# A decoder of two layers on one core: the last pair's routing and its scatter move behind the attention, the shared experts' operands are loaded inside it, and three of eight shared units run beside the first routed experts

## What is computed

```
x = x + L0_attn(layernorm(x));  x = x + L0_xattn(layernorm(x), ctx)
x = x + L0_ffn(layernorm(x))                      # 8 experts, top 2, and a shared one
x = x + L1_attn(layernorm(x));  x = x + L1_xattn(layernorm(x), ctx, 16 heads of 64)
x = x + L1_ffn(layernorm(x))                      # below

scores = sigmoid(x @ gate.T); choose 4 of 8 groups of 8 experts, then top 8 of 64 experts
xe[e, pos] = x[token]   for the first 256 tokens of each expert e
ye = (silu(xe @ w1.T) * (xe @ w3.T)) @ w2.T                       # hidden size 128
out[token] += 2.5 * weight * ye[e, pos]
shared = silu(x @ shared_gate.T) * (x @ shared_up.T) @ shared_down.T   # hidden size 256
```

## Time and profile before

| | |
|---|---|
| median of 3 runs | 3784.36 us (3773.11 to 3792.74) |
| the profiled execution | 3764.9 us, span 3763.2 us |
| busy | PE 3304.6 us, DVE 1865.9, ACT 1650.9, POOL 846.2 |
| granted TensorE clock, mean | 0.952 |

### The profile page before, as it was taken

How to read it: one execution, slowest core, us unless ns; L and a number is a source line. 1 busy time by engine, 2 the same in 40 slices (tenths; PEclk the granted TensorE clock), 3 DMA queues, 4 the chain that set the end, 5 groups by cost and what they waited for, 6 DMA issues and landing times. The chain is left out here.

```text
span 3763.2 us, 76649 instructions
## 1 busy us (share of the span) xinstructions
PE 3304.6 (88%) x24490; PEld 2470.7 (66%) x24491; DVE 1865.9 (50%) x5115; ACT 1650.9 (44%) x4558; POOL 846.2 (22%) x920
## 2 busy tenths in 40 slices
PE   5999996899999777499996988999999999959882
PEld 4777775666666554277774766777777777746762
DVE  3555553677777642022221663556565665642333
ACT  2555553666666410022221325666656565621220
POOL 0000000000000033133332110132323233241774
PEclk9999998999999888799998999999999999979996
DMA  8400003000000231111112000010000000012885
GB/s 275 114 0 0 0 0 135 11 10 8 10 9 10 88 85 48 19 31 30 29 29 55 0 18 27 16 39 19 18 12 12 15 11 13 10 57 90 225 212 138
DMA packets 152369, 181.52 MB, mean 48 GB/s; under 512 B 46428, under 2 KB 126425, under 8 KB 151276
## 3 DMA queue, kind: packets, MB, share of 16 engines
q1 hardware_dynamic: 102476, 137.64, 12.3%
q0 software_dynamic: 47808, 26.74, 4.4%
q10 hardware_dynamic: 2016, 16.25, 1.0%
HBM read 116.17 MB, written 103.88 MB: 58 GB/s over the span
## 5 line engine op out<-in xcount | busy, mean ns | idle before, releaser
L1203 DVE TENSOR_REDUCE e_nmx<-PS 128x1 f32<-128x361 f32 x416 | 221.2, 532 | 400.4 <-PE PS L1044 384.8
L1554 ACT ACTIVATE b_p<-PS,b_nmx 100x361 f32<-100x361 f32 x512 | 275.5, 569 | 162.4 <-DVE b_nmx L1641 162.4
L847 POOL DMA_INDIRECT slot_rows<-r_row,r_rows_now x256 | 255.7, 999 | 401.2 <-DVE e_p L1210 274.8
L1044 PE MATMUL PS<-e_cT,e_qT 128*128 128x361 f32 x832 | 330.1, 479 | 0.0
L1150 ACT ACTIVATE e_pT<-PS 121x384 f32<-121x384 f32 (+1 forms) x416 | 199.2, 479 | 226.2 <-PE PS L1051 219.4
L1641 DVE TENSOR_REDUCE b_nmx<-PS 100x1 f32<-100x361 f32 x512 | 247.5, 526 | 97.6 <-PE PS L1404 95.8
L2509 PE MATMUL PS<-c_wgu,c_tile_xT 128*128 x912 | 290.5, 462 | 1.3 <-ACT c_tile_xT L2564 1.3
L1051 PEld LDWEIGHTS PS<-ident,e_p 128*121 128x121 f32 x1248 | 199.7, 186 | 96.6 <-issue 1.1
L1155 ACT ACTIVATE e_p<-PS,e_nmx 128x361 f32<-128x361 f32 x416 | 232.6, 559 | 69.4 <-DVE e_nmx L1203 67.4
L2754 POOL DMA_INDIRECT sum<-f_y,f_y_token x128 | 198.8, 1553 | 124.0 <-issue 111.6
L1411 PE MATMUL PS<-ident,b_p 100*121 100x100 f32 x1536 | 221.6, 280 | 5.4 <-PEq L181 2.7
(11 more groups left out here) (325 smaller groups left out, 6477.5 us busy)
## 6 DMA issues: line engine op xcount, KB each, us to landing
f_w<-in_f_W SPq DMA_DIRECT2D x64, 384.0 KB
slot_rows<-a_empty SPq DMA_DIRECT2D x1, 21504.0 KB, 65.1
f_xg<-slot_rows SPq DMA_DIRECT2D x64, 336.0 KB
c_wgu<-in_c_GU ACTq DMA_DIRECT2D x8, 1408.0 KB, 19.0
sum<-X SPq DMA_DIRECT2D x2, 3200.0 KB, 57.2
f_sums<-sum SPq DMA_DIRECT2D x16, 400.0 KB
b_cT<-in_ctx_T SPq DMA_DIRECT2D x32, 181.5 KB, 2.3
e_cT<-in_ctx_T SPq DMA_DIRECT2D x32, 181.5 KB, 2.4
```

The lines of the kernel that those rows point to most:

```text
L847: pool.indirect_dma_start(out=self.rows, in_=self.row[:, u, :], in_offset=None, out_offset=bass.IndirectOffsetOnAxis(ap=self.rows_now[:, u ...
L1044: sr.fill_done(pe.matmul(sr.at(f"s{m}", ROWS, CTX), qT[:, at:at + ROWS], cT[:, u, 0:CTX], start=True, stop=True), f"s{m}")
L1203: dve.tensor_reduce(nmx[:, m:m + 1], sr.at(f"s{m}", ROWS, CTX), AX.X, ALU.max, negate=True).then_inc(max_ready, 1)
L1554: sr.move_done(act.activation(p[:, g % 2, a, 0:CTX], sr.at(f"s{g}{a}", S, CTX), ACT.Exp, bias=nmx[:, g, a:a + 1]), f"s{g}{a}")
```

## The change

The last pair's routing moves from the attention's end into the last block, among the first shared units. GpSimd sends pair 14 and pair 15 there, one after the other. The shared weights and seven of the eight units of x are loaded in the attention; the eighth, which needs the last pair, in the last block. Five shared units run before the experts. The other three are cut into four pieces each, and a piece is put beside each of the first 12 experts; the first two turns of experts are written out for it. The shared units use two PSUM banks. Several blocks now share one semaphore that nobody waits for (`k.passed`). In the first cross attention ScalarE waits for SP's four loads of weights before it issues its own.

```
# Routing
     UNITS, BEFORE = B // 4, 5
+        self.sg, self.su, self.sd = sb("sg", ...), sb("su", ...), sb("sd", [128, 2, D])
+        self.sx = sb("sx", [128, self.UNITS - 1, KC, 4 * S])
+    def load_shared(self, sp, shared):
+        for t, src in ((self.sg, shared["G"]), (self.su, shared["U"]), (self.sd, shared["D"])):
+            sp.dma_start(t[:], src.rearrange("(c p) n -> p c n", p=128)).then_inc(self.s_loaded, 16)
+    def load_units(self, sp):
+        sp.wait_ge(self.xT_stored, (B // 2 - 2) * 16 + 16)
+        for j in range(self.UNITS - 1):
+            sp.dma_start(self.sx[:, j], self.xT_rows[:, :, j * 4 * S:(j + 1) * 4 * S])\
+              .then_inc(self.x_loaded[j] if j < self.BEFORE else self.late_loaded, 16)
# packed_cross_attention, SP
                 r.load(sp)
+                r.load_shared(sp, shared)
...
+                r.load_units(sp)
                 r.store_x(sp, bb, TURNS - 2)
-                r.store_x(sp, bb, TURNS - 1)
# GpSimd
                 turn(TURNS - 3, True, False, True, True, False)
-                turn(TURNS - 2, True, False, False, False, False)
# TensorE, ScalarE, VectorE: behind the last turn
-                r.turn_x(pe, bb, TURNS - 1)
-                r.logits(pe, bb, TURNS - 1)
-                r.positions(pe, bb, TURNS - 1)
-                r.move_x(act, bb, TURNS - 1)
-                r.exponent(act, bb, TURNS - 1)
-                bb.wait_moved(dve, TURNS - 2, "y1")
-                r.statistics(dve, TURNS - 1)
-                r.apply(dve, TURNS - 1)
-                for _ in r.choose(dve, bb, TURNS - 1):
-                    pass
# tiled_cross_attention, ScalarE
+                act.wait_ge(loaded, 64)
+                act.wait_ge(loaded, 64)
                 for e in range(8):
                     act.dma_start(ahead_to[:, e].rearrange("p a c n -> p (a c n)"), ahead_from[e])...
# shared_and_experts
+    PIECES, BEFORE, LAST = 4, r.BEFORE, B // 2 - 1
+    BESIDE = -(-PIECES * (UNITS - BEFORE) // Q)
+    ROUTED_X, ROUTED_L, ROUTED_C = 0, 1, 5
+    CHOOSE_AT = {2: 1, 3: 2, 4: 1, 5: 1, 6: 1, 7: 2}
-        sbanks = Banks(k, 0, 6).plan(names)
+        sbanks = Banks(k, 6, 2).plan(names)
+        rb = Banks(k, 0, 1).plan_from(LAST, Routing.PSUM)
+        def beside(n, i):
+            q = BEFORE * PIECES + i * Q + n if isinstance(i, int) and i >= 0 else UNITS * PIECES
+            return divmod(q, PIECES) if q < UNITS * PIECES else (None, None)
# SP
-                for t, src in ((sg, shared["G"]), (su, shared["U"]), (sd, shared["D"])):
-                    sp.dma_start(t[:], src.rearrange("(c p) n -> p c n", p=128)).then_inc(s_loaded, 16)
-                sp.wait_ge(r.xT_stored, B // 2 * 16 + 16)
-                for j in range(UNITS):
-                    sp.dma_start(sx[:, j], r.xT_rows[:, :, j * NB * S:(j + 1) * NB * S]).then_inc(x_loaded[j], 16)
                 for q in range(Q):
                     sp.dma_start(wt[:, q], routed["all"][q]).then_inc(w_loaded[q], 16)
+                r.store_x(sp, rb, LAST)
+                sp.wait_ge(r.xT_stored, LAST * 16 + 32)
+                sp.dma_start(x_last[:], r.xT_rows[:, :, (UNITS - 1) * NB * S:]).then_inc(late_loaded, 16)
                 r.all_sent(sp)
# GpSimd
-                r.copy_rows(pool, B // 2 - 1)
+                r.copy_rows(pool, LAST - 1)
+                layer_norm_rstd(pool, r.ln, LAST)
+                for n in range(2 * r.TOP):
+                    r.send_row(pool, n)
+                r.free_rows(pool, LAST - 1)
+                r.copy_rows(pool, LAST)
                 for n in range(2 * r.TOP):
                     r.send_row(pool, n)
# TensorE (ScalarE and VectorE alike, with shared_gate and shared_rest)
+                for q in range(BEFORE * PIECES):
+                    shared_piece(*divmod(q, PIECES))
+                    if q == ROUTED_X:
+                        r.turn_x(pe, rb, LAST)
+                    if q == ROUTED_L:
+                        r.logits(pe, rb, LAST)
+                    if q == ROUTED_C:
+                        r.positions(pe, rb, LAST)
...
                         if at:
                             widen(*at)
+                        j, part = beside(n, i)
+                        if part is not None:
+                            shared_piece(j, part)
                         if this:
                             narrow(n, i)
-                with pe.Fori(0, TURNS - 1) as i:
+                for i in range(BESIDE):
+                    turn(i, True, True)
+                with pe.Fori(BESIDE, TURNS - 1) as i:
                     turn(i, True, True)
# VectorE
+                r.statistics(dve, LAST)
+                r.apply(dve, LAST)
+                choosing = r.choose(dve, rb, LAST)
+                for q in range(BEFORE * PIECES):
+                    shared_rest(*divmod(q, PIECES))
+                    for _ in range(CHOOSE_AT.get(q, 0)):
+                        next(choosing, None)
```

More of the change, by code:

```diff
@@ L54, in done, with plan_from @@
             self.uses[self.first + b] += turns * self.per[b]
+    def plan_from(self, turn, names):
+        self.plan(names)
+        self.base = [n - turn * per for n, per in zip(self.base, self.per)]
+        return self
     def at(self, name, p, *shape):
@@ L663 @@
     PLACES = 64 * 256
+    UNITS, BEFORE = B // 4, 5
     PSUM = ["rx", "rl", "rc"]
@@ L692, in __init__ @@
         self.copied, self.rows_free = sem("copied"), sem("rows_free")
+        self.sg, self.su, self.sd = sb("sg", [128, KC, 256]), sb("su", [128, KC, 256]), sb("sd", [128, 2, D])
+        self.sx = sb("sx", [128, self.UNITS - 1, KC, 4 * S])
+        self.s_loaded, self.late_loaded = sem("s_loaded"), sem("late_loaded")
+        self.x_loaded = [sem(f"x_loaded{q}") for q in range(8)]
         self.LOADED, self.CONSTANTS, self.STEPS = 32, 4, RANK_STEPS + 25
@@ L918, in packed_cross_attention @@
         at_step = sorted([(n, 0, name) for n, name in own.items()] + [(n, 1, name) for name, n in routed.items()])
-        bb = Ring(k, 7, 1).plan([name for _, _, name in at_step]).ends(TURNS, Routing.PSUM)
+        bb = Ring(k, 7, 1).plan([name for _, _, name in at_step]).ends(TURNS, [])
         def ahead(n, by, i, this, nxt):
@@ L2423, in tiled_experts @@
         gathered = [sem(f"gathered{v}") for v in range(XB)]
-        added, y_free, started = [sem(f"added{v}") for v in range(2)], sem("y_free"), sem("started")
+        added, y_free, started = [sem(f"added{v}") for v in range(2)], sem("y_free"), k.passed
         banks = Banks(k, 0, 6).plan(["g0", "g1", "t0", "t1", "u0", "u1"])
@@ L2766, in _, with shared_piece @@
                 pe.wait_ge(s_loaded, 48)
-                for j in range(UNITS):
-                    pe.wait_ge(x_loaded[j], 16)
-                    for t in range(IT):
+                def shared_piece(j, part):
+                    if part == 0:
+                        if j < BEFORE:
+                            pe.wait_ge(x_loaded[j], 16)
+                        else:
+                            pe.wait_ge(late_loaded, (UNITS - BEFORE) * 16)
+                    if part < IT:
                         for nm, ws in (("g", sg), ("u", su)):
-                            sbanks.wait_free(pe, f"{nm}{t}", j)
+                            sbanks.wait_free(pe, f"{nm}{part}", j)
                             for c in range(KC):
-                                last = pe.matmul(sbanks.at(f"{nm}{t}", 128, NB * S), ws[:, c, t * 128:(t + 1) * 128],
-                                                 sx[:, j, c, :], start=(c == 0), stop=(c == KC - 1))
-                            sbanks.fill_done(last, f"{nm}{t}")
-                    for n in range(NB // 2):
+                                last = pe.matmul(sbanks.at(f"{nm}{part}", 128, NB * S),
+                                                 ws[:, c, part * 128:(part + 1) * 128], (sx[:, j] if j < UNITS - 1 else x_last)[:, c, :],
+                                                 start=(c == 0), stop=(c == KC - 1))
+                            sbanks.fill_done(last, f"{nm}{part}")
+                    else:
+                        n = part - IT
                         sbanks.wait_free(pe, f"y{n}", j, *[f"u{t}" for t in range(IT)])
@@ L2853, in turn @@
                             gate(*at)
+                        j, part = beside(n, i)
+                        if part is not None:
+                            shared_gate(j, part)
                 turn(-1, False, True)
-                with act.Fori(0, TURNS - 1) as i:
+                for i in range(BESIDE):
+                    turn(i, True, True)
+                with act.Fori(BESIDE, TURNS - 1) as i:
                     turn(i, True, True)
@@ L2861, in _, with shared_rest @@
             def _(dve):
-                for j in range(UNITS):
-                    for t in range(IT):
-                        sbanks.wait_moved(dve, j, f"g{t}")
-                        sbanks.wait_full(dve, f"u{t}", j)
```

(18 more changed lines are left out.)

39 lines of the change are left out of this document (23 added, 16 removed).

## The result

The changed kernel takes 3743.6 us (median of 4 runs, 3742.3 to 3746.2) where the kernel before took 3786.8 beside it (3773.1 to 3792.7): ratio 0.9888, 95% interval 0.9862 to 0.9914, 43 us less. The forecast was 3744 us. The sum had said -40.5 us; two of its terms were wrong by 7 to 8 us each, in opposite directions.

What follows compares the result with a forecast made beforehand. Bounds: TensorE nearly idle 31.8 us after the attention's last add, then GpSimd's scatter-adds at 3.88 us an expert. Terms -53.9 + 17.9 - 4.5 = -40.5 us from the 3784.4 median give 3744 us; range 3718 to 3768.

Steps and rivals of the forecast that it cites:

- T: Start of the last block, 0.3 us behind the attention's last add: 3347.8, at the other end 3351.5.
- Loads: Shared weights and seven units of x load inside the attention; the 7.6 us wait goes, no cost on the path.
- GpSimd: Last block's chain: copy, 16 sends to T+24, wait for pair 15's choices, copy, 16 more sends, landing, first gather load.
- VectorE's rows: Pair 15's routing between units 0 and 1: rows ready T+31, first expert's x T+58.5 (bounds T+53, T+67).
- TensorE's chain: Last block before the experts: five units 49.3 us plus pair 15's work, table loads and waiting, T+59; experts start 53.9 earlier.
- Rival B: Code loading: two stalls like the 9.3 us one, in the written out experts; 3762 us; chance 0.19 together with Rival A.
- Three units beside the experts: Pieces beside the first 12 experts make TensorE the bound there: +17.9 us, bounds about 10 and 27.
- The two waits: First cross attention: ScalarE waits for SP's weight loads, first copy near 639; -4.5 us, bounds 0 to -11.
- Rival A: Last block's chain of sends longer: VectorE late, rows at T+45, boundary costs 4 us; 3762; chance 0.19 together with Rival B.
- Rival C: More gain: pieces fill gaps, experts start at T+53, units beside them cost 10 us; 3730 us; chance 0.14.
- Rival D: Slower: TensorE at its lower clock in the first 12 experts, units beside them cost 81 us; 3807 us; chance 0.04.

Runs made afterwards that it cites:

- e2: The kernel before with ScalarE's two waits in the first cross attention put in, nothing else; 3773.8 us against 3784.2, ratio 0.9969.
- e10: The changed kernel with paced exit, six shared units ahead of the experts, and both runs of sends in the last block paced; ratio 0.9874 to the kernel before.

## Why the prediction was right, and where not

1. *T.* 0.28 us behind the add, as said (0.3). T itself is 3349.2 instead of 3343, since the profile's stages before it varied.
2. *Loads.* As said: nothing is waited for.
3. *GpSimd.* Two runs of 16 with a gap: 20.8 us for the first (20.5 said), but 13.0 us from its end to the copy of pair 15's rows and 14.6 to the next send, as the rows were late. The prediction gives this gap twice, 6 to 8 us in its list of signs and 9 by its steps 3 and 4 (T+24 to T+33).
4. *VectorE's rows.* Ready 36 us after T instead of 31; GpSimd's copy of them starts at 3385.36. The 3.3 us stop at 3370.48 and its followers are in this. The sends' chain, as the kernel with four units shows it, ended at T+62 (58.5 said, bounds 53 and 67).
5. *TensorE's chain* is the step that failed in size. The sum was 49.3 us for five units and 9.6 for what comes between. Without sends it measures 52.3 us from T, so the extras cost 3, not 9.6. ScalarE's change to the exponential and back is a part of them, and takes 1.30 us from the start of the load to the next instruction; the load back begins 0.01 us behind that instruction's end. The 2.66 us that the prediction gave for a switch with its drain don't show in these rows:

```profile
3356.30 1.28 ACT L779 ACT_TABLE_LOAD   x1 [1.56 <-PE PS L771]
3357.60 0.28 ACT L779 ACTIVATE r_score<-PS 100x128 f32<-100x128 f32 x1
3357.89 1.28 ACT L2885 ACT_TABLE_LOAD   x1
```

With sends the chain ends at T+67.7, 8.7 us later than said and 15.4 later than without. Laid side by side, TensorE's rows of the two kernels split the 15.4 us: 6.0 are lost before the slow matmuls at 3371.11 begin, 4.2 until unit 1 ends, most of it at the lower clock, and 5.2 by the stop in unit 4. Rival B had named stops of this kind, at 9.3 us each, but put them into the written out experts, where none came, and held against them that the shared units "now run without such a gap". That was read from TensorE alone (busy 73.6 of 81.1 us). ScalarE and VectorE do stop in the second unit of the kernel before:

```profile
3396.22 0.90 ACT L2834 ACTIVATE f_s_gated<-PS 128x400 f32<-128x400 f32 x2 [10.69 <-remote]
...
3394.78 0.69 DVE L2871 TENSOR_TENSOR X<-X,PS 100x512 f32<-100x512 f32 x1 [4.25 <-remote]
```

There ScalarE's input had been waiting for some 4.0 us (its matmuls start at 3390.67), but TensorE lost only 0.9: the unit took 10.79 us (3390.67 to 3401.46) instead of 9.86. It had six PSUM banks to go on with. With two it waits as soon as VectorE is late, 2.90 us for `X` at 3406.23. So the two banks "cost nothing" only while nobody stops: without sends a unit takes 9.86 us (3378.27 to 3388.13) as before, and with sends they pass the stops on to TensorE. Whether six banks would hide the stops in the changed kernel, no run tests. (The prediction counts eight matmul groups in a unit; there are six.) Measured, the first expert came 46 to 47 us earlier (116.0 to 69.0, 116.1 to 70.3), where 53.9 was said.
6. *Three units beside the experts.* +15.8 us (259.1 to 274.9) where +17.9 was said, and about 5 us for each unit from one to four. (The terms that the prediction shows, 63.5 and 8.2, give 71.7 us and +16.9, not 72.7 and +17.9.) An expert with a gate and up piece takes 5.7 us, with an output piece 4.76, so 5.2 on average (5.3 said). Some 11 us of the three units' 27.1 fill time that TensorE had to spare.
7. *The two waits.* -11 to -13 us where -4.5 was said: at the far bound or beyond it. The mechanism was as told, loads that interleave, but the sum charged ScalarE its old 7.54 us of issue behind the last load. Alone it issues the eight in 4.04 us, and the loads before it land after 3.4 us; the first copy came 6 to 8 us earlier by itself. That the stage gives only 4.8 to 6.8 us of the 11 to 13 stays unexplained.

Steps 5 and 6 together: -31 us in the profiles (e2 to after: -46.9 + 15.8) and by the ratios 0.9969 to 0.9888, -30.7 us, where -36.0 was said. Step 7: -11.7 where -4.5 was said. Together -42 to -43. That the forecast of the total was only 0.4 us off is luck: errors of +5 and -7 us cancel, and the rest lies in the median of the kernel before, 3786.8 us beside the changed kernel where the prediction had 3784.4. Rival A's late rows did not come (T+36, not T+45), nor its slow boundary (0.28 us). Rival C did not come either; only the kernel without its sends comes near to it, with experts from T+52.3 and +13.0 us for the three units. Rival D did not come: the granted clock over the experts' stretch was 0.95. It came in small, at 0.50 for 7 us behind the first stop.

## What to carry to other kernels

Where code runs once (the exit of a loop, a block written out), look at GpSimd's sends at that time before putting the stop down to the code: the same exit lost its stop of some 10 us when 12 sends were spread out. A load queue that starts at the same moment as another costs both: the eight large loads went out 3.5 us faster, and the small ones landed 11 us sooner, by waiting. Before a stage gives up PSUM banks, look for stops on the engines that empty them: with six banks a stop of 4.0 us cost TensorE 0.9 us, with two banks stops of 7.7 and 5.6 us cost it 6.0 and 5.2 us. (No run changes the banks alone.) And when a profile lies 0.5% beside its own median, take a second one before pricing stages by differences.

## What the runs showed of the hardware

Beside back-to-back indirect sends of GpSimd (0.30 us between them) ScalarE, VectorE and TensorE stop at some places of code that runs once: VectorE stands idle for 10.8 us at the attention's exit, and ScalarE for some 7.7 and 5.6 us with its input there in units 1 and 4. With gaps of 0.3 to 3.3 us between the sends at the exit, with paced sends in the block (in e10 never more than five in a row less than 0.4 us apart), or without sends in the block, the same code runs on. That sends and their spacing decide it is shown, at two places. Sends alone are not enough: in the kernel with four units the second run of sends (3380.2 to 3400.6) lies beside units 2 and 3, and no engine stops there. That the places are those where new code is needed, and that what is held up is the fetch of instructions, is argued only: the profile has queues for it,

```profile
q8 instruction: 41, 0.67, 0.1%
q14 instruction: 31, 0.25, 0.0%
```

with 16 KB in each packet of the first and 8 KB in those of the second, but in the stretch of the stop (3290 to 3314) the changed kernel shows no packet of either, while the kernel with the paced exit shows one of each between 3302 and 3314. The Trainium skill (Runtime: NRT & Kernel Launch, Instruction fetch mechanics) says that an engine's sequencer fetches code in blocks of 16 KiB through a DMA queue of its own, and that the cost of crossing a block is mostly hidden; the size of the first queue's packets agrees with it. Whether the stops are such a crossing that is not hidden, no run shows. What in a send holds the others up stays open, and so does why the stretch c of one and the same kernel took 215.0 us once and 221.6 us another time; it, too, has "remote" waits beside GpSimd's sends, twelve in the first profile and ten in the second, of up to 25 us.
